# A twelve-layer selective-scan stack on one core: decay factors and states in one set of eleven buffers, and the sum over states taken up five slots back

## What is computed

```
delta = softplus(dtp_w @ dbc[:32] + dtp_b);   B, C = dbc[32:48], dbc[48:64]
h_t = exp(delta_t * A) * h_(t-1) + delta_t * B_t * x_t      # per channel and state
y_t = sum over the 16 states of h_t * C_t,  + x_t * D
out = y_forward * silu(xp) + y_backward * silu(xp) + input
```

## Time and profile before

| what | value |
|---|---|
| median of three runs | 20609.74 us |
| profiled execution, its own time | 20590.7 us |
| its span, first to last instruction | 20588.9 us |
| VectorE busy | 19678.2 us, 96% |
| GpSimd busy | 19541.0 us, 95% |
| TensorE busy | 14397.9 us, 70% |
| ScalarE busy | 11798.2 us, 57% |
| granted TensorE clock, mean | 0.918 |

### The profile page before, as it was taken

How to read it: one execution, slowest core, us unless ns; L and a number is a source line. 1 busy time by engine, 2 the same in 40 slices (tenths; PEclk the granted TensorE clock), 3 DMA queues, 4 the chain that set the end, 5 groups by cost and what they waited for, 6 DMA issues and landing times.

```text
span 20588.9 us, 254528 instructions
## 1 busy us (share of the span) xinstructions
PE 14397.9 (70%) x76320; PEld 9682.2 (47%) x76320; DVE 19678.2 (96%) x11520; ACT 11798.2 (57%) x12601; POOL 19541.0 (95%) x8658
## 2 busy tenths in 40 slices
PE   6676766767676776767767767676776767677676
PEld 4444444444444444444444444444444444444444
DVE  7999999999999999999999999999999999999999
ACT  5555555655556555555655555555565555556554
POOL 7999999999999999999999999999999999999999
PEclk8999999999999999999999999999999999999998
DMA  6667676767667666666767667676676666767666
GB/s 203 216 219 219 220 221 217 220 217 224 216 218 224 215 221 218 218 219 218 224 216 221 218 216 221 216 222 219 218 223 216 219 221 218 221 219 223 215 221 199
DMA packets 1214177, 4494.01 MB, mean 218 GB/s; under 512 B 161408, under 2 KB 172160, under 8 KB 1163392
## 3 DMA queue, kind: packets, MB, share of 16 engines
q1 hardware_dynamic: 1078912, 3934.73, 55.4%
q0 software_dynamic: 82944, 503.35, 12.6%
q10 hardware_dynamic: 50688, 36.88, 0.7%
HBM read 3945.94 MB, written 134.22 MB: 198 GB/s over the span
## 4 chain that ended last, share of the span: by engine, by line
issue 40%; DVE 30%; PE 17%; ACT 5%; POOL 4%; DVEq 1%; DMA 1%; ACTq 1%; POOLq 0%
DVE ring L926 20%; DVE bv L910 9%; PE y L761 6%; PE bank L788 5%; PE bv L751 4%; POOL ring L392 2%; ACT dA L571 2%; DMA c<-c_rows 1%; PE bank L782 1%; ACT tmp L579 1%; ACT bv L571 1%; DVE w L941 1%; PE bank L841 1%; ACT pre L579 1%; ACT pre L583 1%
## 5 line engine op out<-in xcount | busy, mean ns | idle before, releaser
L392 POOL TENSOR_TENSOR ring<-ring,c 128x1024 f32<-128x1024 f32 x6144 | 14689.5, 2521 | 950.3 <-DVE ring L926 613.0
L926 DVE TENSOR_TENSOR_SCAN ring<-dA,bv 128x1024 f32<-128x1024 f32 x4992 | 11199.2, 2273 | 209.4 <-ACT dA L571 62.4
L571 ACT ACTIVATE dA<-delta,a_step 128x1024 f32<-128x1024 f32 x4992 | 5606.4, 1145 | 3232.9 <-DVE ring L926 2914.7
L751 PE MATMUL bv<-parts,select 128*128 128x512 bf16 x9984 | 3307.0, 416 | 5533.2 <-DVE ring L926 5522.0
L761 PE MATMUL y<-ident,ring 128*128 128x128 f32 x49152 | 6923.1, 292 | 171.9 <-POOL ring L392 170.5
L761 PEld LDWEIGHTS y<-ident,ring 128*128 128x128 f32 x49152 | 6343.1, 153 | 1377.1 <-POOL ring L392 320.4
L910 DVE TENSOR_TENSOR bv<-u,bv 128x1024 f32<-128x1024 f32 x4992 | 5944.6, 1214 | 525.9 <-PE bv L751 504.2
L751 PEld LDWEIGHTS bv<-parts,select 128*128 128x128 bf16 x9984 | 706.1, 101 | 7496.1 <-DVE ring L926 7087.7
L571 ACT ACTIVATE bv<-delta,a_step 128x1024 f32<-128x1024 f32 x1152 | 1287.3, 1117 | 3381.3 <-DVE ring L926 3381.1
L402 POOL TENSOR_TENSOR v<-u,v 128x1024 f32<-128x1024 f32 x1152 | 2855.8, 2479 | 0.0
L926 DVE TENSOR_TENSOR_SCAN ring<-bv,v 128x1024 f32<-128x1024 f32 x1152 | 2608.6, 2264 | 0.9
(11 more groups left out here) (71 smaller groups left out, 10215.2 us busy)
## 6 DMA issues: line engine op xcount, KB each, us to landing
c<-c_rows SPq DMA_DIRECT2D x6144, 512.0 KB, 4.8
v<-c_rows SPq DMA_DIRECT2D x1152, 512.0 KB, 5.3
w<-pre POOLq DMA_DIRECT2D x96, 1024.0 KB, 12.3
xf<-tmp POOLq DMA_DIRECT2D x96, 1024.0 KB, 10.9
delta<-pre POOLq DMA_DIRECT2D x96, 1024.0 KB, 8.0
delta<-tmp POOLq DMA_DIRECT2D x96, 1024.0 KB, 10.1
pre<-out_dram SPq DMA_DIRECT2D x88, 1024.0 KB, 7.1
out_dram<-z POOLq DMA_DIRECT2D x96, 512.0 KB, 10.2
```

The lines of the kernel that those rows point to most:

```text
L392: nc.gpsimd.tensor_tensor(ring[k % NR][:], ring[k % NR][:], c_sb[k % NC][:], ALU.mult).then_inc(p_ready, 1)
L571: nc.scalar.activation(to[:], delta_of(d, s)[:, c, :], ACT.Exp, scale=a_step[s][:, c, n:n + 1]).then_inc(da_ready, 1)
L751: mm = pe.matmul(bv[k % 2][:, half(h)], select[:, n:n + 1].to_broadcast([P, P]), parts_of(d, s)[:, half(h)], start=True, stop=True)
L926: nc.vector.tensor_tensor_scan(h, a, b, 0.0, ALU.mult, ALU.add).then_inc(h_ready, 1)
```

## The change

The three `dA` and eight `ring` buffers become eleven buffers `tile`. ScalarE writes exp(delta*A) of tile k into `tile_of(k)`, the scan writes its states over it, GpSimd multiplies it in place, and TensorE sums it. So the exp now waits for the sum (`summed`) of the tile that had the buffer before, 10 or 11 tiles back (31 for tile 30), and no longer for a scan 3 to 5 back. The scan of an own tile has no wait on `summed` any more; that of a SHARED tile keeps one, 10 or 11 back where it was 8. `LAG` goes from 4 to 5. `SEED`, the offset of the counts, goes from 8 to 11.

```diff
-    NDA, NR, NC, NV = 3, 8, 4, 2
-    SEED = 8
+    NB_TILE, NC, NV = 11, 4, 2
+    SEED = 11
...
-    LAG, HELD = 4, 6
+    LAG, HELD = 5, 6
...
-        dA = [sb(f"dA{i}", [P, T]) for i in range(NDA)]
-        ring = [sb(f"ring{i}", [P, T]) for i in range(NR)]
+        tile = [sb(f"tile{i}", [P, T]) for i in range(NB_TILE)]
...
+        CYCLES = (10, 10, 11, 11, 11, 11)
+        assert sum(CYCLES) == TILES and max(CYCLES) == NB_TILE
+        PLACE = [i for n in CYCLES for i in range(n)]
+        def tile_of(k):
+            return tile[PLACE[k]]
+        def gap(k):
+            return next(g for g in range(1, TILES + 1) if PLACE[(k - g) % TILES] == PLACE[k])
...
-                    act.wait_ge(h_ready, tiles(it, k + 1 - da_gap(k)))
-                    to = dA[da_of(k)]
+                    act.wait_ge(summed, tiles(it, k + 1 - gap(k)))
+                    to = tile_of(k)
...
-                dve.wait_ge(summed, tiles(it, k + 1 - NR))
+                h = tile_of(k)[:]
                 if k in SHARED:
+                    dve.wait_ge(summed, tiles(it, k + 1 - gap(k)))
                     dve.wait_ge(vp_ready, others(it, k + 1))
                     a, b = bv[k % 2][:], v_sb[SHARED.index(k) % NV][:]
                 else:
                     dve.wait_ge(v_ready, own(it, k + 1))
-                    a, b = dA[da_of(k)][:], bv[k % 2][:]
-                h = ring[k % NR][:]
+                    a, b = h, bv[k % 2][:]
```

More of the change, by code:

```diff
@@ L391, in product @@
                 pool.wait_ge(c_loaded[k % NC], it * (16 * TILES // NC) + (16 * (k // NC) + 16))
-                nc.gpsimd.tensor_tensor(ring[k % NR][:], ring[k % NR][:], c_sb[k % NC][:],
+                nc.gpsimd.tensor_tensor(tile_of(k)[:], tile_of(k)[:], c_sb[k % NC][:],
                                         ALU.mult).then_inc(p_ready, 1)
@@ L760, in add_up @@
                 for q in range(CHUNKS):
-                    mm = pe.matmul(y[:, chunk(q)], ring[k % NR][:, chunk(q)], ident[:], is_transpose=True,
+                    mm = pe.matmul(y[:, chunk(q)], tile_of(k)[:, chunk(q)], ident[:], is_transpose=True,
                                    start=(k % HALF_TILES == 0 and q % (CHUNKS // NH) == 0),
```

## The result

The changed kernel takes 20558.5 us, median of 17 runs (20536.24 to 20583.0); the kernel before takes 20600.92 us, median of 17 runs (20580.68 to 20621.27). The ratio is 0.9982, 95% interval 0.9974 to 0.9989. The change makes the kernel about 0.2% faster, 42 us. The forecast was 0.1% (20591 us) in a range of 20480 to 20700; it started from a median of three runs of the kernel before that is 9 us above the one here, so its gain was 19 us.

The account below looks back on a forecast made before the run. VectorE, 96% busy, was taken to pace everything, its idle time mostly waits for TensorE's `rep_b`. 20590.7 less 15 to 20 gave about 20572 us profiled; that execution lay 19 us below the median, so 20591 us, range 20480 to 20700.

Parts of the forecast that it names:

- The waits for GpSimd at tile 63: TensorE's slot 60: LAG 5 sums an older product, so VectorE waits less at tile 63; gain 15 to 20 us.
- The moved sums: TensorE's slots 4 and 36 each gain a sum, 7 and 39 lose one: free, 0 us.
- a rival that needed the clock up in every image: TensorE's clock stays up through slot 6, waits at tiles 7 and 9 go: 116 us gained, 20475 us; chance 0.13.
- The slower rival: Idle stretches at slot 63 merge, clock falls over slots 0 to 3: tile 5 loses 112 us, 20703 us; chance 0.17.
- The exp's new gate: ScalarE's exp waits for a sum 10 or 11 tiles back, usually earlier: 0 us, at best all 62.4 us.
- The scan in place: VectorE's scan writes over its input: taken as 0, bounds 45 us up or down; slower-scan rival 20636 us, chance 0.04.
- The scan's dropped wait: Ahead of VectorE's scan, a wait already met is dropped: 0 us, at best some of 147 us.

Follow-up runs that it names:

- the one with the fill in slot 5: Changed kernel plus 28 transposes of the identity, computing nothing, in TensorE's slot 5: 20458.39 us, ratio 0.9929.
- those with five fills: LAG 5 on the old buffers, and the changed kernel, each with identity transposes in slots 5, 19, 43, 49, 51: 1.6% under the kernel before.

## Why the prediction was right, and where it was not

The direction, the range and the case (a small gain, by way of TensorE's timing and not of ScalarE's) held. The size did not come from where the forecast had it. Point by point:

- *The waits for GpSimd at tile 63.* Forecast 15 to 20 us; the wait fell from 31 to 5 us. The mechanism was right for the long waits: all 9 of over 1 us (15.4 us) stood behind a wait for GpSimd in slot 60, and none is left. The rest stood behind a sum at half clock, mostly with no wait for GpSimd, in 39 images before, 21 in the change and 48 with LAG 5 alone. So what went beyond the forecast is where the slow stretches fell, which was luck: LAG 5 alone keeps 17 to 18 us at tile 63. TensorE's waits for products at its sums went from 170.5 us to 2.2, where I had said under 40.
- *The moved sums.* "Free" was the step that failed. Where slot 4's sum itself ran at half clock, it shortened the idle stretch to 2.95 us, and `turn_back` ran at least partly at full clock, in 45 images. I had left this to a rival that needed the clock up in every image (-116 us). Where the sum ran at full clock the stretch was 4.21 us, as estimated, and `turn_back` stayed slow. What came lies between the two: `finish` -35 us, but tile 9 +21 us, since the clock now falls under the sums there.
- *The slower rival.* Its mechanism came: the two idle stretches at slot 63 became one of 4.09 us, and the clock falls at the start of the image. Its sign was wrong. The fall comes so early that it is over by slot 2, and tile 5 gained 46 us where I had put a loss of 112. LAG 5 alone shows the same 42 us, the buffers alone 95, so it is LAG that does it.
- *The exp's new gate.* Right in both directions: no wait for an exp outside the 11 layer edges (47.9 us; the 17.4 us that the profile puts down to ScalarE are the stops at tile 14), and no gain from ScalarE being free.
- *The scan in place.* Right, 0 (2274 ns and 2273).
- *The scan's dropped wait.* Taken as 0, with 147 us as its bound. It is worth 32 us, of which 21 came back as stops at tile 14. What it did to TensorE's slow stretches was not foreseen at all.
- *Not foreseen*: the stops behind the loop edge, 31 us at tile 13.

The terms outside tile 63 were -35, -46, -27 and -24 (tiles 40 and 41), against +21, +31, +22, +21 and +9; together they give 28 us where I had 0, so the forecast owes its closeness to their opposite signs, which is luck.

I had said that I would be wrong if the wait before `times_b` moved by over 60 us (it moved by 12), or if `finish` no longer waited (it waits half as long).

## What to carry to other kernels

Where a matrix engine feeds a full engine in small pieces and idles in between, look at the granted clock in the pieces that have no time to spare; work that computes nothing, put into the idle stretch ahead of such a piece, was worth 1.4% here, nearly seven times the change. A fill must still end before the next needed piece when the work ahead of it ran at half clock, and its output must go to a buffer that no one reads at the time. Such gains depend on where the slow stretches fall, and an edit that computes nothing seems to have moved the time by some 25 us here; so a difference of that size between two such kernels says little about the edit itself. When two edits come together and the profile says that only one acts, measure that one alone: here it was the better kernel.

## What the runs showed of the hardware that was not expected

- Transposing fp32 matmuls, 28 of them with nothing else in slot 5, held the granted clock at 1.00 through slots 5 and 6, where it was 0.50 after an idle stretch of 5.08 us.
- A longer idle stretch can be the better one, if the clock falls and is up again before the slot that needs it: 2 long waits at tile 5, not 31.
- TensorE stops for up to 3.6 us in the first slot of its loop in a third of the images (32 stops, 50 us). It shows as "issue", moves with the loop's edge, and comes only where a jump back was taken. The kernel before has 2 such stops, the eleven buffers alone none, the one with the fill in slot 5 has 9, of 9 us in all, and those with five fills have 0 and 1; why so few was not tried.
- A wait instruction that is already met costs the scan behind it some 0.03 us (a step of 0.132 us and not 0.103, 32 us over some 1100 places).
